# Layer 2's points by node groups in turn, and layer 3's sums and image sums on 64 rows each, with the 65th column apart

## The chip, the core and the metric

The kernel runs on one core of a Trainium2 chip. The core has five engines that work side by side, each with its own queue of instructions in fixed order: TensorE (PE, matrix products; PEld is its loading of weights), VectorE (DVE), ScalarE (ACT), GpSimd (POOL) and SyncE (SP), which here only issues DMAs. They meet by semaphores. The metric is the device time of one execution in microseconds, as the median of the runs.

## What is computed

Four graph layers run one after the other over the same 4096 nodes of 64 features and the same 4096 x 4096 matrix `adj`, which has about 0.4% nonzero entries but is handled as a full one. Between layers there is a layer norm with a ReLU and a residual sum. The code counts the layers from 0; the title's second layer is `_L1`, its third `_L2`.

```python
def _L0(h, adj):                       # layer 0
    return relu((adj @ h) @ W.T + b)

def _L1(x, adj):                       # layer 1: attention on a hyperboloid
    h = lorentz_linear(x, W, b, scale) # a "point": time = sigmoid(z0)*exp(scale)+1.1,
    q = lorentz_linear(h, Wq, ...)     #   the rest of the row scaled by
    k = lorentz_linear(h, Wk, ...)     #   sqrt((time*time-1) / sum of squares)
    att = sigmoid((2 + 2 * minkowski(q, k)) / att_scale + att_bias)
    support = (adj * att) @ h
    return support / sqrt(|inner(support)|)

def _L2(x, adj):                       # layer 2: Poincare ball
    log_ij = logmap(x_i, x_j)          # for every pair of nodes
    agg = sum_j adj[i, j] / deg_i * log_ij
    return expmap(0, agg @ weight + bias)

def _L3(x, adj):                       # layer 3: weights 2**-(rank of the neighbour)
    return (mask * 0.5 ** (k - pos)) @ (x @ weight) + bias
```

## The kernel before, in words

A tile is 128 nodes (`T` = 32 tiles). Node groups `g` = 0 and 1 are 16 tiles each; they share instructions of 128 x 1024 elements (16 tiles of 64 features).

**Layer 0 and the passage to layer 1.** For each half of the columns (`h`) and each tile of `adj_t`, TensorE (`tile0`) adds the tile's part of `adj @ h` (four f32 products on 64 array columns each, output rows 0 to 63 and 64 to 127 in turn) and counts nonzero entries for layer 3; VectorE makes the mask (`mask0`) and adds up the degrees (`degree0`, into `TB`); ScalarE turns the counts into bytes (`make_code`) and stores them. Then comes a serial passage. `update0(1)` adds the second half of layer 0's result to `X`; `norm_stats` and `norm_out` normalize both groups; `flip` turns features on TensorE, `flipped_out` copies them; `linear` multiplies with the weights; `lorentz_squares` (ScalarE), `lorentz_ratio`, `lorentz_root` and `lorentz_point` make the points h, then q, then k, each time for both groups. `high`, `key_low` and GpSimd's subtraction split q and k into two f16 parts; `fold` and `fold_both` turn these on TensorE and copies bring them back. `degrees` sums the degrees on TensorE, with idle products (`keep_at_work`) between.

**The score loop** has 64 steps `s` of two halves `u`: `scores` (TensorE), `sigm` (ScalarE), `product` with `adj` (VectorE) and `gather1` (TensorE), which adds the product's 128 x 1024 numbers into 64-row sums, again on 64 array columns in turn. Some of the folding and copying for group 1 is set into its first steps.

**Layer 2** works on 72 units `(S, p)`: a strip `S` of 512 nodes against a pair `p` of tiles (256 nodes). The distance is symmetric, so 56 units are *mirrored*: they serve the node sums of both sides. In unit n, `scores2` makes the products (f32, two row halves of the array) and `sides2` adds side terms (four row groups); ScalarE squares (`square2`), takes logarithm and two exponentials (`roots2`) and a last logarithm (`arc2`); VectorE makes `rest2`, `sum2`, `pair2`; GpSimd multiplies with `adj` (the *near* part); for a mirrored unit TensorE transposes the pair factors (`mirror2`) and VectorE multiplies these with the other block of `adj` (`far2`). The sums weight each node's row `Zn` of 65 numbers (64 features and a time part): `gather2_near` adds 2 products of 512 columns over the strip, kept in PSUM for the strip's length and brought out by `near2_out`; `gather2_far` adds 4 products of 256 columns, brought out after each unit by `far2_out` into the image `GA` (65 rows). `nodes2` turns the image back to nodes by products with the identity, 32 in all, in three groups of 8, 8 and 16 tiles; the last group comes inside layer 3's loop.

TensorE's order by iteration n is `scores2(n+1)`, `sides2(n)`, `mirror2(n-1)`, then the sums of unit n-2. VectorE's is `far2_out(n-3)`, `near2_out(n-3)` where a strip ends, `sum2(n)`, `far2(n-1)`, `rest2(n+1)`, inserted steps of the next or last passage, `pair2(n)`. ScalarE's is `roots2(n)`, inserted steps, `square2(n+1)`, `arc2(n)`. This order is written out by hand. Loads of `adj` blocks run five units ahead and wait for the sums of unit n-5.

**Layer 3** steps 64 times over the stored bytes: `power` on ScalarE and VectorE, 12 bf16 passes on TensorE (`step3`); the end of layer 2 for the last 16 tiles is set into its steps (`last_passage3`).

An f32 product is two passes of TensorE in the trace (a weight load and a stream each); a plain f32 transpose is one.

## Time and profile before

| | us |
|---|---|
| median of 3 runs | 1091.84 |
| lowest and highest run | 1090.72, 1092.6 |
| the profiled execution | 1090.43 |
| its span, from first to last instruction | 1088.7 |
| TensorE busy in the span | 1036.7 |
| VectorE busy | 862.8 |
| ScalarE busy | 767.5 |

A busy time is the time in which at least one instruction of the engine runs, so two products at once count once. The chain of waits goes back from the last instruction to what released it, and again from there. By it layer 0 ends at about 250 us, the first score product starts at 304.77, the units of layer 2 run from about 553 to 971, and the rest is layer 3.

### The profile page before, as it was taken

Reading aid. Unit: us, or ns where it says so; the run is one execution under the profiler, and the core shown is the slowest. Engines: PE = TensorE matmul, PEld = TensorE weight load, DVE = VectorE, ACT = ScalarE, POOL = GpSimd, SP = SyncE. Lnnn points to the kernel's source line nnn. Section 1 sums busy time; section 2 is a strip of 40 time slices with the busy share of each in tenths; the row PEclk is TensorE's granted clock in tenths of the full one; section 3 lists DMA queues with packets and bytes.
Section 4 is the critical chain, followed back from the end, with each engine's and each line's share of the span. In section 5 each row is a group of like instructions: output and inputs, shape, how many; then the busy total and the mean of one; then the engine's idle time right before and its main releaser. Section 6 shows DMA issues by size and latency. Waiting matters only on the chain.

```text
span 1088.7 us, 14887 instructions
## 1 busy us (share of the span) xinstructions
PE 1036.7 (95%) x5430; PEld 448.2 (41%) x5430; DVE 862.8 (79%) x1013; ACT 767.5 (71%) x807; POOL 270.7 (25%) x140
## 2 busy tenths in 40 slices
PE   7999999999789999999979999999999998989998
PEld 2333333336633333334324443444554554436544
DVE  7999989996766666697669987887789887898781
ACT  5555455553556656676688899988888888997682
POOL 1089500000010000003015364434343433440010
PEclk9999999999989999999999999999999999999999
DMA  9989989980048888778754445555455545446451
GB/s 353 396 343 423 393 322 346 359 331 30 2 154 274 280 290 280 247 274 288 245 180 136 135 135 175 177 172 193 155 168 181 170 140 174 136 140 208 140 173 40
DMA packets 96341, 238.32 MB, mean 219 GB/s; under 512 B 16400, under 2 KB 45072, under 8 KB 79888
## 3 DMA queue, kind: packets, MB, share of 16 engines
q1 hardware_dynamic: 87056, 220.62, 58.3%
q10 hardware_dynamic: 9216, 16.78, 4.0%
q8 instruction: 43, 0.70, 0.3%
q14 instruction: 26, 0.21, 0.1%
HBM read 219.55 MB, written 17.83 MB: 218 GB/s over the span
## 4 chain that ended last, share of the span: by engine, by line
PE 74%; DVE 12%; ACT 9%; issue 4%; DMA 1%; SPq 0%; DVEq 0%; ACTq 0%
PE PS L563 51%; PE PS L737 5%; PE PS L738 5%; PE PS L870 4%; PE PS L839 4%; ACT work L1224 2%; ACT work L1232 2%; DVE work L1969 2%; DVE work L1957 1%; ACT work L1235 1%; DVE ring L1975 1%; DVE work L1963 1%; ACT work L1218 1%; PE PS L575 1%; ACT work L1155 1%
## 5 line engine op out<-in xcount | busy, mean ns | idle before, releaser
L1637 DVE TENSOR_TENSOR work<-work,ring 128x1024 f32<-128x1024 f32 x128 | 151.2, 1223 | 76.8 <-ACT work L1155 76.7
L1155 ACT ACTIVATE work<-PS,att_sc 128x1024 f32<-128x1024 f32 x128 | 147.7, 1202 | 85.7 <-PE PS L738 78.4
L1090 ACT ACTIVATE work<-PS 128x1024 uint8<-128x1024 f32 x128 | 124.0, 1020 | 107.6 <-PE PS L563 107.6
L563 PE MATMUL PS<-ring,work 128*65 128x256 f32 (+1 forms) x600 | 191.8, 467 | 4.1 <-DVE work L1996 4.0
L541 POOL TENSOR_TENSOR ring<-work,ring 128x1024 f32<-128x1024 f32 x57 | 135.9, 2384 | 236.6 <-DVE work L1969 236.5
L563 PE MATMUL PS<-work 128*64 128x512 f32 (+2 forms) x800 | 153.6, 526 | 1.1 <-ACT work L1218 1.0
L1963 DVE SCALAR_TENSOR_TENSOR work<-PS,work 128x1024 f32<-128x1024 f32 x72 | 88.0, 1223 | 53.8 <-PE PS L563 45.3
L563 PEld LDWEIGHTS PS<-ring,work 128*65 128x65 f32 x600 | 80.8, 139 | 91.5 <-issue 66.0
L737 PE MATMUL PS<-work 128*128 128x512 f16 x256 | 98.9, 386 | 2.0 <-DVE work L1444 1.3
L1224 ACT ACTIVATE work<-work 128x1024 f32<-128x1024 f32 x72 | 76.0, 1055 | 34.8 <-DVE work L1957 34.7
L738 PE MATMUL PS<-work 128*128 128x512 f16 x256 | 98.2, 384 | 0.0
L1969 DVE SCALAR_TENSOR_TENSOR work<-work 128x1024 f32<-128x1024 f32 x72 | 87.9, 1221 | 2.3 <-ACT work L1239 1.8
L563 PEld LDWEIGHTS PS<-work 128*64 128x64 f32 (+2 forms) x800 | 38.2, 119 | 120.7 <-issue 112.3
L839 PE MATMUL PS<-TB,TA 64*128 64x512 f32 x288 | 81.6, 643 | 2.6 <-DVE work L1963 2.6
L1239 ACT ACTIVATE work<-work 128x1024 f32<-128x1024 f32 x72 | 75.8, 1053 | 9.1 <-DVE work L1963 6.8
L563 PE MATMUL PS<-work,TB 128*64 128x512 bf16 x672 | 76.4, 384 | 2.1 <-DVE work L1952 2.1
L1232 ACT ACTIVATE work<-work 128x1024 f32<-128x1024 f32 x72 | 76.1, 1057 | 2.3
L563 PE MATMUL PS<-work,tri_above 128*128 128x512 bf16 x256 | 75.8, 379 | 0.0
L1235 ACT ACTIVATE work<-work 128x1024 f32<-128x1024 f32 x72 | 75.0, 1042 | 0.0
L870 PE MATMUL PS<-ident,work 128*128 128x128 f32 x448 | 62.0, 282 | 13.3 <-DVE work L1969 12.5
L563 PE MATMUL PS<-work,tri_rest 128*128 128x512 bf16 x248 | 74.4, 382 | 0.0
L1500 DVE TENSOR_TENSOR TB<-TB,work 128x2048 f32<-128x2048 f32 x32 | 74.2, 2318 | 0.1
(267 smaller groups left out, 1479.9 us busy)
## 6 DMA issues: line engine op xcount, KB each, us to landing
ring<-in_adj_t SPq DMA_DIRECT2D x96, 1024.0 KB, 5.3
ring<-in_adj_t SPq DMA_DIRECT2D x104, 512.0 KB, 3.8
work<-in_adj_t SPq DMA_DIRECT2D x32, 1024.0 KB, 8.3
codes<-work ACTq DMA_DIRECT2D x64, 256.0 KB, 7.4
ring<-codes SPq DMA_DIRECT2D x64, 256.0 KB, 3.7
H<-in_adj_t SPq DMA_DIRECT2D x24, 512.0 KB, 3.9
X<-in_x SPq DMA_DIRECT2D x2, 256.0 KB, 4.5
X<-in_x SPq DMA_DIRECT2D x1, 512.0 KB, 9.9
```

The lines of the kernel that those rows point to most:

```text
L541: nc.gpsimd.tensor_tensor(near(n), sums(n), near(n), ALU.mult).then_inc(sem("near_ready"), 1)
L563: return mm(out_ap, lhsT, rhs, start=starts, stop=True, skip_group_check=True)
L737: mm(o, k_hl[:, jt * P:(jt + 1) * P], q_hh[:, i0:i0 + BANK], start=True, stop=False)
L738: ins = mm(o, k_hl[:, jt * P:(jt + 1) * P], q_ll[:, i0:i0 + BANK], start=False, stop=True)
L839: mm(z_banks(n)[:, q * BANK:(q + 1) * BANK], TA[half_rows(q), p * P:(p + 1) * P], TB[half_rows(q), S * STRIP:(S + 1) * STRIP], start=True, ...
L870: ins = nc.tensor.transpose(PS[:, c:c + P], sums(n)[:, q * BANK + i * P:q * BANK + (i + 1) * P], ident[:, :])
L1090: nc.scalar.activation(made[:, k, u * UNIT:(u + 1) * UNIT], PS[:, (4 + 2 * u) * BANK:(6 + 2 * u) * BANK], ACT.Relu).then_inc(sem("codes_ma ...
L1155: nc.scalar.activation(att[:, u, :], PS[:, (4 + 2 * u) * BANK:(6 + 2 * u) * BANK], ACT.Sigmoid, bias=att_sc[:, 2:3], scale=att_sc[:, 1:2]) ...
L1232: nc.scalar.activation(sums(n), lnr[:, n % ROT, :], ACT.Exp, scale=0.5).then_inc(sem("root_ready"), 1)
L1637: V.tensor_tensor(prob[:, m % 4, :], att[:, u, :], ring[:, s % RING, u * UNIT:(u + 1) * UNIT], ALU.mult)\
L1963: V.scalar_tensor_tensor(sums(n), z_banks(n), 1.0, sums(n), ALU.max, ALU.add)\
L1969: V.scalar_tensor_tensor(sums(n), sums(n), TAU_MAX, lnr[:, n % ROT, :], ALU.min, ALU.mult)\
```

## The change

**First part.** Layer 0's second half gets its second block of eight tiles written out, and the normalization of group 0 for layer 1 (`sums_l1`, `centre_l1`, `spread_l1`, `feats_l1`) is set between its tiles; it writes into `cen` and is flipped right after the last tile. The points then go group by group in the order h0, h1, q0 with k0, q1 with k1 (`POINTS`), with statistics of their own for k. The degrees are summed in one go. The first scores wait for q0 and k0 alone. What is left of k1 (factor, point, rounding, low part, fold) and q1 is put into steps 1 to 14 of the score loop; q1's products are copied out of PSUM first (`zq_out`).

**Second part.** The near sums use output rows 0 to 63 and the far sums rows 64 to 127, in one routine that alternates them and waits for both parts first. The 65th column is summed by products with a single weight column, near on output rows 0 and 32 and far on rows 64 and 96, into the second half of PSUM bank 3. `far2_out` and `near2_out` have two pieces each. The node images are added up by a product with two identities one above the other (`stacked`), and the 65th column of each tile by one or two products with one column of the identity. Group 1's turned left rows go through bank 0 in place of bank 3.

```diff
+            nc.gpsimd.tensor_tensor(stacked[:, :], ident[:, 0:D], ident[:, D:P], ALU.add).then_inc(sem("consts_ready"), 1)
...
+            pe.wait_ge(sem("feats_ready_l1"), 1)
+            flip(cen, 0, 0).then_inc(sem("flipped"), 1)
             pe.wait_ge(sem("sums_out0_v"), 1)
             to_nodes(wbd["l0"][:, :], UNIT, 2, 0).then_inc(sem("z0_ready"), 1)
 
             pe.wait_ge(sem("codes_made"), 4 * T)
+            pe.wait_ge(sem("flip_out"), 1)
+            linear(wbd["l1"][:, :], 1, 0, 4).then_inc(sem("lin_h"), 1)
             pe.wait_ge(sem("deg_added"), 2 * T)
...
+            degrees(7, 6)
+            for _ in range(4):
+                keep_at_work(6)
+            pe.wait_ge(sem("feats_ready_l1"), 2)
+            flip(H, 1, 0).then_inc(sem("flipped"), 1)
+            pe.wait_ge(sem("feats1_ready"), 1)
+            flip(HL, 0, 0).then_inc(sem("flipped"), 1)
             pe.wait_ge(sem("deg_out"), 1)
...
+            pe.wait_ge(sem("flip_out"), 2)
+            linear(wbd["l1"][:, :], 1, 1, 4).then_inc(sem("lin_h"), 1)
+            pe.wait_ge(sem("flip_out"), 3)
+            linear(wbd["q"][:, :], 2, 0, 4).then_inc(sem("lin_q"), 1)
+            linear(wbd["k"][:, :], 3, 0, 0).then_inc(sem("lin_k"), 1)
+            for _ in range(8):
+                keep_at_work(2)
+            pe.wait_ge(sem("feats1_ready"), 2)
+            flip(HL, 1, 0).then_inc(sem("flipped"), 1)
+            pe.wait_ge(sem("flip_out"), 4)
+            linear(wbd["q"][:, :], 2, 1, 4).then_inc(sem("lin_q"), 1)
+            linear(wbd["k"][:, :], 3, 1, 0).then_inc(sem("lin_k"), 1)
...
-                if s == 0:
+                if s == 5:
                     fold_both(1)
-                if s == 4:
+                if s == 10:
                     pe.wait_ge(sem("khl_out"), 2)
+                    fold_high(1, 2)
+                if s == 13:
+                    pe.wait_ge(sem("qhh_out"), 2)
                     fold_low(1, 2)
...
                 if n == AUX_L:
-                    pe.wait_ge(sem("far_out"), mirrors(n - 1))
-                    turn_left(1, 3)
+                    pe.wait_ge(sem("aux_r_out_a"), 2)
+                    turn_left(1, 0)
...
                 if n > AUX_R and mirrors(n) == mirrors(AUX_R) + 1:
-                    pe.wait_ge(sem("aux_r_out_a"), 2)
+                    pe.wait_ge(sem("aux_l_out"), 2)
                     pe.wait_ge(sem("aux_r_out_v"), 2)
...
+                if mirrored(n):
+                    pe.wait_ge(sem("far_ready"), mirrors(n))
+                if mirrors(n) - mirrored(n) > 0:
+                    pe.wait_ge(sem("far_out"), mirrors(n) - mirrored(n))
                 for q in range(2):
-                    ins = add(PS[0:D + 1, 2 * BANK:3 * BANK], Zn[:, 2 * p + q, 0:D + 1], near(n)[:, q * BANK:(q + 1) * BANK],
-                              opens(n) and q == 0)
-                ins.then_inc(sem("agg2_near"), 1)
-
-            def gather2_far(n):
+                    add(PS[half_rows(0), 2 * BANK:3 * BANK], Zn[:, 2 * p + q, 0:D], near(n)[:, q * BANK:(q + 1) * BANK],
+                        opens(n) and q == 0)
+                    if mirrored(n):
+                        for i in (2 * q, 2 * q + 1):
+                            add(PS[half_rows(1), 3 * BANK:LAST], Zn[:, S * ST + i, 0:D], far(n)[:, i * PAIR:(i + 1) * PAIR], i == 0)
+                for q in range(2):
+                    if mirrored(n):
+                        last_far2(n, 2 * q)
+                    for c in range(2):
+                        ins = add(PS[32 * c:32 * c + 1, LAST:LAST + PAIR], Zn[:, 2 * p + q, D:D + 1],
+                                  near(n)[:, q * BANK + c * PAIR:q * BANK + (c + 1) * PAIR], opens(n) and q == 0)
+                    if q:
+                        ins.then_inc(sem("agg2_near"), 1)
+                    if mirrored(n):
+                        ins = last_far2(n, 2 * q + 1)
+                        if q:
+                            ins.then_inc(sem("agg2_far"), 1)
+
+            def last_far2(n, i):
                 S, p = UNITS[n]
...
+                for c in range(2):
+                    ins = add(PS[64 + 32 * c:65 + 32 * c, LAST:LAST + P], Zn[:, S * ST + i, D:D + 1],
+                              far(n)[:, i * PAIR + c * P:i * PAIR + (c + 1) * P], i == 0)
+                return ins
...
                 for t in range(*GROUPS[q]):
-                    ins = mm(PS[:, agg2_col(t):agg2_col(t) + D + 1], GA[0:D + 1, t * P:(t + 1) * P], ident[0:D + 1, 0:D + 1],
-                             start=True, stop=True)
+                    r, to = (P, stacked) if t >= ST else (D, ident)
+                    mm(PS[:, agg2_col(t):agg2_col(t) + D], GA[0:r, t * P:(t + 1) * P], to[0:r, 0:D], start=True, stop=True)
+                    for k, (r, rows) in enumerate(last_rows(t)):
+                        ins = add(PS[:, agg2_col(t) + D:agg2_col(t) + D + 1], rows, ident[:, r:r + 1], k == 0)
...
+            flipped_out(0, 0)
+            lorentz_squares("h", 4, 0)
+            one("ln_sq", grp(sqr, 1), grp(cen, 1), ACT.Square, ("ln_centred", G + 3))
+            power_of("ln_sd", st[2], st[1], -0.5, "ln_var", G + 2, (1,))
+            lorentz_roots(("h", 0))
+            flipped_out(0, 1)
+            flipped_out(1, 0)
+            lorentz_squares("h", 4, 1)
+            lorentz_squares("q", 4, 0)
+            lorentz_roots(("h", 1))
+            lorentz_squares("k", 0, 0)
+            flipped_out(1, 1)
+            lorentz_roots(("q", 0), ("k", 0))
+            lorentz_squares("q", 4, 1)
+            lorentz_squares("k", 0, 1)
+            high("q", HBq(0), Q2(0), 0)
+            high("k", HBk[0], grp(K2, 0), 0)
             folded_out("qhh_out", q_hh, 0, 4, "qhh_ready")
...
+            lorentz_sum("h", 1)
+            lorentz_ratio(("h", 1))
+            lorentz_sum("q", 0)
+            feature_point(1)
+            lorentz_sum("k", 0)
+            lorentz_ratio(("q", 0), ("k", 0))
...
                 if s == 1:
+                    lorentz_factor(("k", 1))
+                    key_point(0, 1)
+                if s == 3:
+                    key_low(1)
+                if s == 6:
                     keys_out(1)
-                if s == 4:
+                if s == 7:
+                    lorentz_factor(("q", 1))
+                    query_point(1, HBq(1))
...
+                    V.tensor_tensor(at, at, got, ALU.add)
+                    V.tensor_tensor(last, last, last_got, ALU.add).then_inc(sem("far_out"), 1)
```

## Rows read from the trace of the kernel before

**Rows 1.** The page's first part: busy us (share), instructions, of each engine.
```profile
PE 1036.7 (95%) x5430; PEld 448.2 (41%) x5430; DVE 862.8 (79%) x1013; ACT 767.5 (71%) x807; POOL 270.7 (25%) x140
```

**Rows 2.** Busy times by stretch; window: length, each engine, clock, DMA share, GB/s.
```profile
158.00:250.00 92.00, 92.00 (x400) 29.45 (x397) 85.89 (x50) 47.95 (x51) 0.00 (x0) 1.00 0.88 325
250.00:305.00 55.00, 42.54 (x385) 36.24 (x384) 37.85 (x108) 27.20 (x44) 2.27 (x2) 0.93 0.02 6
574.00:635.00 61.00, 59.62 (x271) 27.55 (x271) 57.42 (x79) 52.76 (x58) 31.29 (x22) 0.98 0.46 147
635.00:690.00 55.00, 50.11 (x280) 22.62 (x279) 41.93 (x47) 52.07 (x54) 27.70 (x13) 0.97 0.47 154
690.00:771.00 81.00, 81.00 (x391) 39.54 (x390) 63.91 (x76) 70.18 (x71) 33.22 (x14) 1.00 0.54 177
771.00:911.00 140.00, 138.02 (x684) 70.77 (x682) 116.30 (x163) 118.23 (x129) 54.21 (x25) 1.00 0.50 162
971.00:1088.00 117.00, 106.50 (x904) 58.42 (x902) 77.49 (x127) 77.78 (x91) 7.87 (x3) 0.99 0.44 145
```

**Rows 3.** The chain of waits in one mirrored unit: start us, us, what.
```profile
689.28 3.44 PE PS L563 x12
692.72 1.06 PE PS L839 x4
693.78 0.33 PE PS L563 x4
694.11 1.02 PE PS L870 x8
```

**Rows 4.** The chain of waits in the passage to the scores, and one ScalarE copy.
```profile
283.26 0.91 PE PS L597 x8
284.19 1.02 ACT work L1118
285.24 1.20 DVE st L1559
...
286.61 0.32 DVE time_q L1566 x2
...
301.58 1.88 PE PS L715 x16
303.49 1.24 DVE work L1444
304.77 0.61 PE PS L737
...
299.86 1.86 ACT L1043 ACTIVATE work<-PS 128x2048 f16<-128x2048 f16 x1
```

**Rows 5.** Groups by shape: score loop on VectorE and ScalarE; busy, mean ns, idle before.
```profile
L1637 DVE TENSOR_TENSOR work<-work,ring 128x1024 f32<-128x1024 f32 x128 | 151.2, 1223 | 76.8 <-ACT work L1155 76.7
L1155 ACT ACTIVATE work<-PS,att_sc 128x1024 f32<-128x1024 f32 x128 | 147.7, 1202 | 85.7 <-PE PS L738 78.4 <-DVE work L1637 7.1
```

**Rows 6.** Instructions in time on TensorE: one tile's sums in layer 1.
```profile
390.62 1.94 PE L563 MATMUL PS<-work 128*64 128x512 f32 x8
```

**Rows 7.** Instructions in time on ScalarE: first step of two following units.
```profile
681.17 1.06 ACT L1224 ACTIVATE work<-work 128x1024 f32<-128x1024 f32 x1 [0.22 <-DVE work L1957]
686.34 1.06 ACT L1224 ACTIVATE work<-work 128x1024 f32<-128x1024 f32 x1 [0.22 <-DVE work L1957]
```

**Rows 8.** Groups by shape: VectorE bringing out far and near sums.
```profile
L1985 DVE TENSOR_TENSOR work<-work,PS 65x256 f32<-65x256 f32 x42 | 17.3, 411 | 4.4 <-PE PS L563 4.4
L1996 DVE TENSOR_TENSOR work<-work,PS 65x512 f32<-65x512 f32 x11 | 7.5, 679 | 0.4
```

**Rows 9.** TensorE: one-column products in time, then the last node images in the chain.
```profile
270.47 1.62 PE L662 MATMUL PS<-ones,TB 128*128 128x1 f32 x14
...
982.26 3.72 PE PS L957 x32
```

**Rows 10.** Waits from 965 us on: who waited for whom, total us, times, longest.
```profile
ACT work L1246 <- PE PS L957: 3.1, 1, 3.1
```

More of the change, by code:

```diff
@@ L213, in graph_layers @@
         HL = nodes(slot(5))
-        HBk = nodes(slot(7))
+        HBk = [work[:, k * UNIT:(k + 1) * UNIT].rearrange("p (t c) -> p t c", t=TG) for k in (14, 6)]
         def HBq(g):
@@ L698, in fold, with fold_high @@
                 return ins
-            for g in range(G):
+            def fold_high(g, dst):
                 pe.wait_ge(sem("q_high"), g + 1)
-                fold(Q2, 0, g, 4 + 2 * g).then_inc(sem("qhh_ready"), 1)
+                fold(Q2, 0, g, dst).then_inc(sem("qhh_ready"), 1)
             def fold_low(g, dst):
@@ L980, in _ @@
                 if n >= 2:
[L981 to L983 removed]
+                    gather2(n - 2)
                 if n in FLIPS:
@@ L1213, in second_half2 @@
                 if n == AUX_L + 1:
-                    one("aux_l_out", aux_l[:, UNIT:2 * UNIT], banks(3, 4).bitcast(BF16), ACT.Copy, ("aux_turned", 4))
+                    one("aux_l_out", aux_l[:, UNIT:2 * UNIT], banks(0, 1).bitcast(BF16), ACT.Copy, ("aux_turned", 4))
             def square2(n):
@@ new lines, in lorentz_factor @@
+            def lorentz_factor(*points):
+                for n, (tag, g) in enumerate(points):
+                    ratio, root, factor = (grp(v, g) for v in TAGS[tag][2:5])
+                    dve.wait_ge(sem("point_root"), nth(tag, g))
+                    chained(n, V.reciprocal(factor, root))
+                for n, (tag, g) in enumerate(points):
+                    ratio, root, factor = (grp(v, g) for v in TAGS[tag][2:5])
+                    hold(n)
+                    chained(n, V.tensor_tensor(factor, factor, ratio, ALU.mult))
+                for n, (tag, g) in enumerate(points):
+                    ratio, root, factor = (grp(v, g) for v in TAGS[tag][2:5])
+                    hold(n)
+                    chained(n, V.tensor_tensor(factor, factor, root, ALU.add))
```

296 lines of the change are left out of this document (158 added, 138 removed).

## The prediction

> **What bounds the kernel now.** I read the page's engine line first: TensorE is busy 95% of the span [rows 1]. A busy share says little where stages differ, so next the busy times by stretch [rows 2], then in each stretch what is late last. The end of layer 0 (158 to 250 us) has TensorE without a gap and VectorE at 85.89 of 92. Between 250 and 305 us nothing is full: a serial passage. From 574 to 635 TensorE (59.62 of 61) and VectorE (57.42) are both nearly full. From 635 to 690 ScalarE is (52.07 of 55). From 690 to 771 TensorE alone is (81.00 of 81). From 771 to 911 TensorE again, with VectorE near it in parts. The last layer starts near 971 and TensorE leads there too.
>
> One unit of layer 2 is visible in the chain of work [rows 3]: sums 3.44 us, distance products 1.06, side terms 0.33, mirror transposes 1.02, together 5.85. Nothing else stands in that chain.
>
> **Part one, the passage from layer 0 to the scores.** Today the chain runs from about 250.2 to the first score product at 304.77 [rows 4], 54.5 us. Prices [rows 4]: a full-size vector step 1.20 to 1.22 (reduce, scaling), a pair of 16-column steps 0.32 (I take 0.2 for a lone one), a ScalarE pass 1.02, a bank of products 0.91 and some 0.2 of bias ahead (I take 2.4 for a group of two banks with its latency), a fold 1.88 on a TensorE that has just idled (I take 1.0 on one that has not), a copy of folded rows 1.24 on VectorE and 1.86 on ScalarE. The new order, step by step: flip of the features of group 0, then second half of layer 0's products, 3.3 (ends 253.5). Update, mean, centring of group 1, the sum of h0, spread of group 1: five full steps and a little, 6.3 (259.8). Ratio of h0 (seven small steps) 1.6, reciprocal root 0.8, features 1.2, factor 0.7, point 1.4: 5.9 (265.7). Flip of group 1, copy, product 4.7 (270.4). Square, sum, ratio, sum of q0, factor, point of h1: 7.2 (277.6). Flip, copy, products of q1 and k1: 6.8 (284.4). ScalarE squares k1 before it rounds q0, so that waits: square, rounding, fold, copy 5.1 (289.5). Low parts and key fold with copies 3.4 (292.9). The chain is 42.7 us, 11.8 less; with folds at 1.88 each 2 less gain. I take 11. What leaves the chain runs inside the score loop: a fold on TensorE, which is full there, costs 1.0. The vector steps (factor and point, 2.2 at tiles 1 and 7, low part 1.2) and ScalarE's (roundings 1.0, copy 1.9) meet idle times of 76.8 and 85.7 us over 64 tiles [rows 5], 1.2 and 1.3 a tile, and two of four product buffers in hand: nothing. Without that cover each would cost its own length, about 9 in all.
>
> The normalization of group 0 moves into layer 0's second half: four full vector steps and six small, 6.2 us, into 6.1 us of vector idle time [rows 2]. The masks run over two tiles ahead of TensorE, about 8 us, so a lag of 5 is not felt; behind it stand only the releases of eight load buffers. I take nothing, at worst 2. The constant added on GpSimd comes before TensorE's first work, which still waits later for features. **Sum: -10, between -6 and -12.**
>
> **Part two, a mirrored unit's sums.** 56 of the 72 units are mirrored. Today 12 passes (each f32 product is two), 4096 columns, one after the other: 3.44 us, 0.84 ns a column [rows 3]. New: near on array columns 0 to 63 and far on 64 to 127. In layer 1 sums of just that form, 8 passes of 512 columns, take 1.94 in place of 3.44 [rows 6], so pairs run at once, four slots of 0.43 with a tail. So 1.72 to 1.93 here, since the two sides have unequal passes. The 65th column: near 8 passes of 256, far 16 of 128, on four column groups. If four run at once 8 x 256 x 0.84 / 2 = 0.86; if one after the other 3.44; if two at once 1.72. Nearest are the side terms, four products at once on four row groups in 0.33 [rows 3]: I take 0.9 to 1.1. The side terms stream 512 two-byte columns each, which at half the f32 price is 0.22, and take 0.33 [rows 3]: I charge the 0.1 to the change of array form, and there are two more such changes in the new unit.
>
> The Trainium skill, TensorEngine Tiling (Restrictions), states that changing the tiling mode drains the engine, which speaks against this change; the 0.1 above is what the trace shows of it, and it is in the sum. By TensorE: Matmul & The Clock Gate (Part 3) three column groups gave 2.38 times, which for the 65th column would be an estimated 0.86 x 3 / 2.38 = 1.08.
>
> Together 2.8 to 3.3, taken as 3.0: a unit on TensorE goes from 5.85 to 5.4. The next limit is the ring sum, far product, root argument on VectorE, then logarithm and root on ScalarE: where TensorE isn't late, ScalarE's first step recurs after 686.34 - 681.17 = 5.17 us [rows 7]. So the gain can't pass 0.68 a unit.
>
> **Its costs.** VectorE takes a second piece out for each. 65x256 takes 411 ns and 65x512 679 [rows 8]: 1.05 ns a column, so 0.28 for 128, and 0.21 queued; 0.3 for the near side. An unmirrored unit's sums grow from 1.72 by 0.86 and two changes of form, 1.3 with the seams. The merged sums wait for near, far and the former far output at once; all three are done during the products and transposes ahead, and behind the wait stand only the next unit's products. At unit 14 the turned rows now leave over bank 0, so a mirror waits for one more ScalarE copy: 1.0 once. The node images: 32 passes take 3.72 now, 0.116 each, and one-column passes take the same, 14 in 1.62 [rows 9], since they load 128 columns of weights. A tile past the fourth needs six passes in place of two: the groups grow by 2.8, 3.7 and 7.4.
>
> **By stretch** [rows 2]. 574 to 635: VectorE gets 10 x 0.21 + 0.3 on 57.42 and has 3.6 idle, partly TensorE's doing: +0.5. 635 to 690: unmirrored sums six times 1.3 on a TensorE with 4.9 idle, plus the copy: +2.5. 690 to 771: 81 / 5.85 = 14 units x 0.45: -6.3. 771 to 911: TensorE -0.45 x 22 + 2.8 + 3.7 = -3.4, VectorE 22 x 0.21 + 0.6 = +5.2 where its extra steps make it last: -1. 911 to 971 has both kinds of unit, six of each kind, and no engine far ahead: 0. Tail: the last two units are unmirrored, 2.6, and the last images 7.4. ScalarE already waits 3.1 for those images [rows 10], TensorE's following steps queue behind them, and TensorE is 106.50 of 117 there, so nothing covers: +10. **Sum: +5.7**, between -2 and +10.
>
> **Total.** -10 + 5.7 = -4.3 on 1088.7 of span, 1090.43 with what lies around it: 1086.1. The runs' median 1091.84 is 1.4 above the profiled execution; the same difference on the median gives 1087.5.
>
> **Rivals.** (1) *The array doesn't run the 65th column's four groups at once.* The trace has no one-column product on column groups. At 1.72 to 1.85 for it a unit takes 6.2 to 6.4: some 45 mirrored units that are TensorE's +0.4 to +0.5, -10 + 10 + 20 + 3 (unmirrored) and the images' 6.5 partly: about 1112, slower. It decides from sums of 3.5 us a unit upwards. For it: passes of unequal length, short ones with a load each. Against: [rows 3, 6]. Chance 13%. A page's rule would make it worse: if products start strictly in order and a product's second pass waits for its own columns, near's second pass blocks far's first; the layer 1 sums would then take five slots, 2.15 and its tail, where 1.94 is seen [rows 6]. A unit would take 6.8 and the kernel about 1130; 3%. (That products keep strict order is the Trainium skill, TensorE: Matmul & The Clock Gate, Part 3.)
> (2) *The passage gains half.* ScalarE's queue is in fixed order and serves two groups; each late square or rounding holds the next, and the new chain passes through it seven times. Then -5 in place of -10: 1092.5, no change or slightly slower. 16%.
> (3) *Sums at 2.8 and a TensorE that hasn't slowed at the first scores*: -12, -8.5 and a freer TensorE from 771 on: 1080. 12%.
> (4) Forecast, 1087.5, own range 1083 to 1092: 56%.
>
> **How the numbers follow.** No change is within 0.2% (2.2 us), about what a measurement of this kernel can tell. Of the forecast's 56% I count 41 faster, 10 the same, 5 slower; (3) 12 faster; (2) 2 faster, 7 same, 7 slower; (1) 16 slower. Faster 0.55, same 0.17, slower 0.28. Range 1079 to 1108: it takes in (3), (2) and the milder part of (1).
>
> **What would show it.** First score product at 292.9 to 295, and a score loop of the old length but for one fold. In the steady stretch a period of 5.2 to 5.5 with sums of 2.8 to 3.3; above 3.44, rival 1. The 128-column vector pieces at 0.28. Last node images 11.1. The end of the loop of units earlier by some 14, the total by 4. The prediction is wrong if units get longer, if TensorE waits for masks before 250, or if the tail hides the images.

## The result and the profile after

The changed kernel takes 1110.95 us (median of 4 runs, 1110.51 to 1112.73) where the kernel before takes 1092.22 in the same comparison: a ratio of 1.0175, 95% interval 1.0156 to 1.0193. It is slower by 19 us; forecast was 1087.5. The profiled execution has a span of 1109.3 us, 20.6 more than the span before.

The page of the changed kernel, its first parts (busy us, share of the span, instructions; then TensorE's granted clock, the share of full speed at which the engine was allowed to run, in tenths over 40 slices), to be set against [rows 1]:

```profile
span 1109.3 us, 18109 instructions
PE 1043.4 (94%) x6983; PEld 481.0 (43%) x7002; DVE 887.1 (80%) x1080; ACT 768.6 (69%) x808; POOL 250.1 (23%) x141
PEclk9999999999899999999989999999999899997999
```

No engine's share has moved by more than a point or two, which is why a page of shares can't tell where 20 us went. Milestones can. I took the starts of the first score product, of the last attention product, and, in layer 2, of ScalarE's logarithm of the sums, once per unit (unit n runs from the start before it to its own; the time between is called its period here). The tail is what follows the last of them. From the two traces, in us:

| stretch | before | after | difference | forecast |
|---|---|---|---|---|
| start and layer 0, to the last mask | 239.3 | 242.1 | +2.8 | 0 |
| passage, last mask to first score product | 65.5 | 54.7 | -10.8 | -10 |
| scores to the first unit | 253.9 | 254.3 | +0.3 | 0 |
| units 1 to 24 | 136.8 | 143.5 | +6.7 | +3.0 |
| units 25 to 38 | 82.0 | 73.9 | -8.1 | -6.3 |
| units 39 to 60 | 139.3 | 152.5 | +13.2 | -1 |
| units 61 to 71 | 56.9 | 57.3 | +0.4 | 0 |
| tail | 115.0 | 131.0 | +16.0 | +10 |

The loop of units was to end some 14 us earlier. Its last logarithm starts 4.6 us later (978.3 after, 973.7 before).

Both gains are there. The steady mirrored unit has a period of 5.17 us in place of 5.85. TensorE's lines in time of one such unit after (start us, us, instruction), to be read against [rows 3]:

```profile
697.32 1.09 PE L903 MATMUL PS<-ident,work 128*128 128x128 f32 x8
698.34 2.92 PE L591 MATMUL PS<-ring,work 128*64 128x512 f32 x36
701.19 1.13 PE L872 MATMUL PS<-TB,TA 64*128 64x512 f32 x4
702.25 0.39 PE L591 MATMUL PS<-work 9*128 9x512 bf16 x4
702.58 1.09 PE L903 MATMUL PS<-ident,work 128*128 128x128 f32 x8
703.60 2.71 PE L591 MATMUL PS<-H,work 128*64 128x512 f32 x28
```

The sums take 2.85 us from their start to the start of the distance products, where they took 3.44. The products of the 64 features take 1.88 of it, and the 65th column 0.97, from 700.22 on; two groups at a time would be 1.72 by the prediction's count. In the trace the first products on its four column groups start at 700.217, 700.223, 700.230 and 700.237, so the four do run side by side. The largest losses lie elsewhere: in the node images. Their stretches after, by windows (length, then busy us of each engine with instructions, granted clock, DMA share, GB/s), are the first group's, the second's, the last's, and the 25 us behind the last:

```profile
770.40:775.90 5.50, 5.50 (x42) 5.18 (x38) 1.49 (x3) 2.83 (x3) 2.36 (x1) 0.91 0.63 194
877.20:883.70 6.50, 6.50 (x50) 6.50 (x46) 2.29 (x4) 3.02 (x3) 2.36 (x1) 0.77 0.50 161
989.20:1006.10 16.90, 16.90 (x99) 16.86 (x97) 3.35 (x6) 0.00 (x0) 0.00 (x0) 0.62 0.52 169
1006.10:1031.00 24.90, 24.90 (x201) 13.92 (x202) 18.83 (x39) 20.15 (x27) 0.00 (x0) 0.91 0.39 124
```

and in the kernel before the last group's, whose end [rows 9] also show:

```profile
982.20:986.00 3.80, 3.80 (x36) 3.73 (x36) 3.28 (x6) 0.72 (x1) 0.00 (x0) 1.00 0.83 257
```

TensorE has no gap in any of them, and yet its granted clock averages 0.62 in the last. The tiles in time show the fall itself (changed kernel, last images; two products of 64 columns, four of one column, for each tile):

```profile
991.93 0.41 PE L1006 MATMUL PS<-stacked,work 128*128 128x64 f32 x2
992.18 0.56 PE L591 MATMUL PS<-ident,TA 128*128 128x1 f32 x4
992.60 0.41 PE L1006 MATMUL PS<-stacked,work 128*128 128x64 f32 x2
992.85 0.56 PE L591 MATMUL PS<-ident,TA 128*128 128x1 f32 x4
...
994.51 0.67 PE L1006 MATMUL PS<-stacked,work 128*128 128x64 f32 x2
994.97 0.96 PE L591 MATMUL PS<-ident,TA 128*128 128x1 f32 x4
995.79 0.67 PE L1006 MATMUL PS<-stacked,work 128*128 128x64 f32 x2
```

A tile takes 0.67 us (six passes of 0.112) up to 993.3 and 1.28 behind it: from 2.4 to 1.2 GHz. The images take 16.9 us in all, where 16 tiles at 0.67 would be 10.7.

### The profile page after: what moved, and what is told of

It is laid out like the page before. It is cut to its first block, busy times and chain, and to the rows that moved or that the text cites. A ratio compares the mean times of both kernels' runs of the same rounds, so it can differ in the third digit from the quotient of the medians.

```text
span 1109.3 us, 18109 instructions
## 1 busy us (share of the span) xinstructions
PE 1043.4 (94%) x6983; PEld 481.0 (43%) x7002; DVE 887.1 (80%) x1080; ACT 768.6 (69%) x808; POOL 250.1 (23%) x141
## 4 chain that ended last, share of the span: by engine, by line
PE 55%; issue 21%; POOL 13%; DVE 5%; ACT 4%; DMA 1%; POOLq 0%; SPq 0%; DVEq 0%; ACTq 0%
PE PS L591 39%; POOL ring L569 10%; PE PS L767 5%; PE PS L768 5%; POOL H L569 2%; ACT work L1213 1%; PE PS L603 1%; DVE work L2095 1%; DMA X<-in_x 1%; PE PS L625 1%; PE PS L1006 1%; PE PS L694 0%; DVE work L2089 0%; PE PS L725 0%; PE PS L919 0%
## 5 line engine op out<-in xcount | busy, mean ns | idle before, releaser
L591 PE MATMUL PS<-ring,work 128*1 128x128 f32 (+3 forms) x1800 | 172.9, 369 | 6.5 <-DVE TA L2114 3.1
L591 PEld LDWEIGHTS PS<-ring,work 128*1 128x1 f32 (+1 forms) x1800 | 89.3, 102 | 82.5 <-issue 53.5
L591 PEld LDWEIGHTS PS<-work 128*64 128x64 f32 (+2 forms) x800 | 38.2, 119 | 121.0 <-issue 112.2
L1282 ACT ACTIVATE work<-PS 128x1024 f32<-128x1024 f32 x72 | 72.6, 1009 | 5.0 <-PE PS L591 4.9
```

Source lines behind the costliest of these rows:

```text
L591: return mm(out_ap, lhsT, rhs, start=starts, stop=True, skip_group_check=True)
```

## The experiments

Each kernel ran against the kernel before, which took 1092.62 to 1093.63 us in these later comparisons; the ratios are to that. Periods below are in us; they are those of the profiled execution. A unit's period repeats from one kernel to the next within some 0.03 us where nothing touched it and the clock is the same (unit 4 is an exception, below), so single units can be compared. "39+40" and "55+56" hold the first two groups of images and the unit behind each.

| kernel | time | ratio, interval | 1-24 | 25-38 | 39+40 | 55+56 | tail |
|---|---|---|---|---|---|---|---|
| before | 1092.22 | | 136.8 | 82.0 | 13.44 | 13.13 | 115.0 |
| changed | 1110.95 | 1.0175 (1.0156-1.0193) | 143.5 | 73.9 | 18.59 | 20.14 | 131.0 |
| passage_only | 1083.71 | 0.9911 (0.9887-0.9935) | 137.7 | 81.9 | 13.44 | 13.14 | 113.4 |
| sums_only | 1124.38 | 1.0294 (1.0277-1.0311) | 142.6 | 73.9 | 18.94 | 20.13 | 131.1 |
| merged_images | 1092.66 | 0.9994 (0.9978-1.001) | 143.8 | 73.9 | 13.81 | 13.27 | 122.7 |
| dense_images | 1138.98 | 1.0421 (1.0403-1.0439) | 143.8 | 73.9 | 25.43 | 25.50 | 143.1 |
| held_images | 1105.49 | 1.012 (1.0087-1.0154) | 143.8 | 73.9 | 21.82 | 17.02 | 125.4 |
| merged_no_adds | 1086.76 | 0.9948 (0.9928-0.9967) | 142.2 | 73.5 | 13.88 | 13.21 | 120.9 |
| merged_turn | 1091.74 | 0.9987 (0.9967-1.0007) | 141.9 | 73.9 | 16.58 | 13.27 | 121.0 |
| merged_x1 | 1089.22 | 0.9976 (0.9945-1.0008) | 141.6 | 73.9 | 15.17 | 13.27 | 121.1 |
| passage_held | 1081.81 | 0.9883 (0.9857-0.9908) | 137.6 | 81.9 | 13.45 | 13.13 | 113.4 |
| passage_held_long | 1081.17 | 0.9885 (0.9867-0.9903) | 136.6 | 81.9 | 13.44 | 13.14 | 113.4 |

**The two parts alone.** passage_only has the new order of the second layer's points and nothing of the sums. None of its lines for the units of layer 2 differs from the kernel before.

> The kernel before with the second layer's points by groups alone; the third layer's sums, image sums and the turn of unit 14 as before. In the changed kernel the first score product came 10.9 us earlier counted from the last mask of layer 0, and the last attention product of layer 2 came 7.7 us earlier than before; layer 0 itself and the kernel's start were 2.8 us longer together. My theory: this part is a gain of its own and is kept to the end, as the rest follows it without slack: 1092.2 - 7.7 = 1084.5 if the lost 2.8 us belong to it, 1081.7 if they belong to the other part (ratio 0.990 to 0.993). Rival: the gain is given back behind the scores, as the units of the third layer meet a VectorE that still has the moved work: 1089 to 1092. In layer 0 I expect the extra 1.7 us to show here (the normalization's steps between the masks), and the first 1.1 us not to.

sums_only is the reverse: every line on the 65th column, `stacked`, and the turn into bank 0.

> The kernel before with the other part alone: third layer's sums and image sums on 64 rows each, with the 65th column apart, and the turn of unit 14 into the other bank. If the two parts add up, this is 1111 + 8 = 1119 (ratio 1.024 to 1.027), with the steady period of the units at 5.17 us, the unit of the first image group at 12.1 us and the last image group at 16.9 us, as in the changed kernel. Rival: the loss in the changed kernel came from the two parts together (the moved points of layer 2 against the first units of layer 3): then this is under 1110.

passage_only came out as the theory had it: 1083.71, ratio 0.9911. sums_only is far from its rival, but at 1124.38 it is 5 us over the 1119 expected, and its ratio of 1.0294 lies above the range given. Its profiled execution, the shortest of its four (1121.54 us), has the expected periods and last images of 17.3 us; why the other three took 1124 to 1125 no profile shows. Multiplied, the parts give 0.9911 x 1.0294 = 1.020 beside 1.0175, which agree within their intervals. The passage is a gain of 9 us, the sums are a loss of 32. One more expectation fell: the 1.7 us of layer 0 were to show in passage_only and not in sums_only. From first to last mask the trace of before has 227.7 us, the changed one 229.4, passage_only 230.4, and sums_only, which touches nothing in layer 0, 229.2. merged_turn, which has the new layer 0, has 227.7 again. So most of the 2.8 us at the start is the spread of executions, not the change.

**The images' products.** merged_images lets near row and far row of a tile share a block of columns; in the gather the two near rows take alternate tiles, and the images read both values, for two tiles, with one product:

```diff
-                        ins = add(PS[32 * c:32 * c + 1, LAST:LAST + PAIR], Zn[:, 2 * p + q, D:D + 1],
-                                  near(n)[:, q * BANK + c * PAIR:q * BANK + (c + 1) * PAIR], opens(n) and q == 0)
+                        ins = add(PS[32 * c:32 * c + 1, LAST:LAST + PAIR].rearrange(...), Zn[:, 2 * p + q, D:D + 1],
+                                  every_other(near(n)[:, q * BANK:(q + 1) * BANK], c), opens(n) and q == 0)
...
-                    for k, (r, rows) in enumerate(last_rows(t)):
-                        ins = add(PS[:, agg2_col(t) + D:agg2_col(t) + D + 1], rows, ident[:, r:r + 1], k == 0)
+                    if t % 2:
+                        ins = add(PS[:, at:at + D + 2:D + 1], GU[p // NS][:, p % NS * P:(p % NS + 1) * P], stacked[:, 0:D:32], True)
```

> The changed kernel with the 65th column laid out so that the near row and the far row of a tile share one block of columns; a pair of tiles then gets its two values of the column from one product with two columns, in place of eight passes of one column. My theory: the one-column products of the images let TensorE's granted clock fall to half (0.77 and 0.70 in the two units with images, 0.50 in most of the last group, 0.82 to 0.91 in the units behind). Three passes per tile at 0.116 us and the clock held: last group 5.6 us in place of 16.9, first group's unit with its follower 5.4 us shorter, second 7.0 us shorter: 1111 - 23.7 = 1087.3 (range 1085 to 1091), granted clock 1.00 in these units. Rival: the number of passes alone counts and the clock falls as before, since one-column products are left: each of the losses is halved: 1111 - 12 to 13 = 1098. Rival: the images aren't the cause: 1108 to 1111.

Measured 1092.66, 18 us less than the changed kernel, where the theory had 23.7 and the first rival 12 to 13. That lies between the two and above the theory's range of 1085 to 1091. Windows of its three groups of images:

```profile
776.80:779.90 3.10, 3.10 (x29) 2.92 (x25) 1.54 (x3) 2.87 (x3) 2.11 (x1) 1.00 0.53 163
878.50:881.20 2.70, 2.70 (x28) 2.66 (x24) 2.32 (x4) 2.67 (x3) 0.93 (x1) 1.00 0.50 139
983.30:991.10 7.80, 7.80 (x52) 7.76 (x50) 3.37 (x6) 0.00 (x0) 0.00 (x0) 0.70 0.93 297
```

The first two groups hold the full clock and their units with followers shrink by 4.8 and 6.9 us, as expected (5.4 and 7.0). The last took 7.8 and not 5.6: its clock fell to 0.70. It has few one-column products left, so "one-column products" was too narrow a name for the cause. The passage took 60.7 us in the profiled execution in place of 54.7 (below), and the median seems to carry some of that: of its ten executions the five with a mean clock of 0.980 to 0.983 took 1093.8 to 1096.7 us, the five with 0.986 or 0.987 took 1088.8 to 1091.5. In all four profiles of kernels with merged images the last group fell (6.4 to 8.0 us up to the next product), and in two of them the first group's stretch did as well (39+40 of 16.58 and 15.17 us). So merging makes the fall rarer and shorter and doesn't end it.

**Which work holds the clock.** dense_images repeats each product of 64 columns:

```diff
-                    mm(PS[:, agg2_col(t):agg2_col(t) + D], GA[0:r, t * P:(t + 1) * P], to[0:r, 0:D], start=True, stop=True)
+                    for _ in range(3):
+                        mm(PS[:, agg2_col(t):agg2_col(t) + D], GA[0:r, t * P:(t + 1) * P], to[0:r, 0:D], start=True, stop=True)
```

> The changed kernel with each 64-column image product issued three times in a row (the same value written again), the one-column products as they are. More work of TensorE, only denser. My theory (the clock falls for lack of dense work): at full clock a tile takes 0.67 + 0.43 = 1.10 us in place of 1.28 at the lower clock: last group 17.6 us, first two groups' units 14.0 us each, the units behind back at 5.2 us: 1111 to 1113 in all, granted clock at least 0.9 in these units and 1.00 behind them. Rival (the clock falls for another reason, whatever TensorE does there): ten passes at the lower clock, 2.1 us per tile: last group 30 us, in all 1130 or more, with the granted clock as low as in the changed kernel.

The theory in that form was wrong, and the time is the rival's: 1138.98 us. Its last group, by window:

```profile
1009.30:1037.50 28.20, 28.20 (x160) 28.16 (x158) 3.37 (x6) 0.00 (x0) 0.00 (x0) 0.61 0.30 101
```

TensorE's weight loads (second of the busy numbers) fill 28.16 of these 28.20 us. Products of 64 columns are thin too: each loads 128 columns of weights to stream 64. That gave the theory its second form, and the next kernel its test: long products between the tiles, in a corner of a bank that the images leave free (one more stands behind each group).

```diff
                         ins = add(PS[:, agg2_col(t) + D:agg2_col(t) + D + 1], rows, ident[:, r:r + 1], k == 0)
+                    for _ in range(2):
+                        mm(PS[:, spare:spare + PAIR], tri_rest[:, :], tri_above[:, :].unsqueeze(1).broadcast_to([P, 2, P]),
+                           start=True, stop=True)
```

> The changed kernel with two further products of 256 columns and 128 weight rows each behind every tile of the images (their result is used by nobody). In dense_images more products of 64 columns made the stretch longer and the clock lower still (0.60 to 0.69), so my theory in its first form, that the one-column products alone starve the clock, fell. Second form: what starves it is a stretch made of products of 64 columns and fewer, in which TensorE mostly loads weights; long products between them should hold the clock, although they are more work. Then a tile takes 0.67 + 0.21 = 0.88 us at the full clock: last group 14.1 us (16.2 in the changed kernel), first two units with images 12.2 us each (12.1 and 13.0), the units behind them 5.2 to 5.6 us (6.5 and 7.1), granted clock 0.95 or more in all of these: 1111 - 6 = 1105 (range 1102 to 1108). Rival: the clock falls in this stretch whatever is added: a tile takes 1.28 + 0.42 = 1.70 us behind the fall, last group 24 us: 1125 or more.

Measured 1105.49, 5.5 us less than the changed kernel, by a kernel that gives TensorE over 64 products more. Windows of its three groups and of the 25 us behind the last:

```profile
771.00:778.60 7.60, 7.60 (x56) 6.53 (x52) 1.53 (x3) 2.86 (x3) 2.36 (x1) 0.82 0.44 141
881.10:887.20 6.10, 6.10 (x65) 6.01 (x61) 2.28 (x4) 3.00 (x3) 2.37 (x1) 1.00 0.53 172
989.60:1002.10 12.50, 12.50 (x126) 12.29 (x124) 3.35 (x6) 0.00 (x0) 0.00 (x0) 1.00 0.66 229
1002.10:1027.00 24.90, 24.90 (x220) 14.40 (x220) 19.87 (x44) 21.34 (x28) 0.00 (x0) 1.00 0.44 138
```

In the second and last group the clock stays at 1.00 and the stretch gets shorter with more in it (16.9 to 12.5 us). In the first it fell all the same (0.82), and that unit and its follower are 3.2 us longer than in the changed kernel; the dose that is enough isn't settled by these runs. The second form holds in two groups of three. The time fell on the 1105 expected partly by luck: the last group took 12.5 us where 14.1 were given, the first unit with images 14.84 where 12.2 were.

The rival that the clock falls there whatever TensorE does is refuted by the second and last group. What is left of the theory's words needs care, though: weight loads fill 12.29 of the 12.50 us in the last group too, so their busy share doesn't tell a stretch that holds its clock from one that doesn't. What differs between the kernels is the long products between the thin ones.

**VectorE's second pieces.** merged_no_adds drops the additions of the 65th column on VectorE (its products and its first copies stay), so that column of the means is incomplete.

```diff
                     V.tensor_tensor(at, at, got, ALU.add)
-                    V.tensor_tensor(last, last, last_got, ALU.add).then_inc(sem("far_out"), 1)
```

> The kernel with merged images, with the additions of the 65th column into its sums left out on VectorE (48 of 0.29 us and 4 of 0.41 us; its copies and TensorE's products stay), so the 65th column of the third layer's means is not what it should be. Theory: VectorE's second pieces are what made units 4 to 21 and 41 to 51 longer than in the kernel before, since VectorE is busy 93 to 99% there; each piece that ends on the path gives back its 0.29 us: some 25 of them, -7 us against merged_images: 1085.5. Rival: what made these units longer is that the far sums are now taken up only behind the near sums and the other way round (two waits where there was one), and the pieces are hidden: within 2 us of merged_images, 1090 to 1093.

Measured 1086.76, 5.9 us under merged_images (5.0 by the ratios). But of the two traces' difference of 10.2 us, 3.4 lie before the first score product, 2.7 of them in the passage. Counted in periods, units 1 to 24 give 1.6 us (1.15 of it unit 4, which differs from one profile to the next in any case, below), units 41 to 54 give 2.2, mostly 0.2 each, and the tail 1.8, where the last images' clock differed too. So the additions cost about the 0.2 us they were priced at, in the units where VectorE is last, and they are not what made most of units 4 to 21 longer. Neither is the rival shown: these units had other reasons, found in the next two kernels.

**The turn of unit 14.** In the changed kernel, waits from 640 to 645 us (who waited for whom, total us, times, longest):

```profile
PE PS L903 <- ACT work L1091: 2.3, 1, 2.3
DVE H L2101 <- PE PS L903: 2.0, 1, 2.0
```

The mirror waits for ScalarE's copy out of bank 0, and VectorE for the mirror. merged_turn gives that copy to VectorE:

```diff
-                if n == AUX_L + 1:
-                    one("aux_l_out", aux_l[:, UNIT:2 * UNIT], banks(0, 1).bitcast(BF16), ACT.Copy, ("aux_turned", 4))
...
+                if n == AUX_L + 1:
+                    copy_out("aux_l_out", aux_l[:, UNIT:2 * UNIT], banks(0, 1).bitcast(BF16), ("aux_turned", 4))
                 sum2(n)
```

> The kernel with merged images, with the copy of the turned side vectors of unit 14 made by VectorE ahead of the sum of unit 15, in place of ScalarE behind its other work. The turn now lies in bank 0, where the next unit's mirror is written, so in the changed kernel the mirror of unit 15 waited for ScalarE's copy until 643.58 us and VectorE stood idle 1.96 us before it could take it. Theory: this wait is the whole of what the move of the turn costs: units 14 to 16 together go from 19.06 us to 17.1 to 17.6 us (the kernel before has 17.12 us), and the time from 1092.7 to 1091. Rival: the three units are longer for VectorE's further pieces, and the copy on VectorE adds its 0.68 us: 19.1 to 19.7 us, 1092.7 to 1093.3.

Units 14 to 16 take 6.58 + 5.27 + 5.55 = 17.40 us where merged_images has 19.05, inside the theory's 17.1 to 17.6: the wait was 1.65 us of the stretch. The time, 1091.74, is within the noise of 1092.66.

**GpSimd and VectorE.** In unit 6 the period rose from 5.89 to 7.32 us. VectorE and GpSimd there, changed kernel:

```profile
581.24 2.37 POOL L533 TENSOR_TENSOR X<-X,work 128x1024 f32<-128x1024 f32 x1
581.79 2.37 DVE L2083 TENSOR_SCALAR work<-work 128x1024 f32<-128x1024 f32 x1
```

and the same two operations in the kernel before, with the next one of VectorE:

```profile
587.69 4.14 POOL L505 TENSOR_TENSOR X<-X,work 128x1024 f32<-128x1024 f32 x1
587.78 0.68 DVE L1957 TENSOR_SCALAR work<-work 128x1024 f32<-128x1024 f32 x1
588.38 1.22 DVE L1969 SCALAR_TENSOR_TENSOR work<-work 128x1024 f32<-128x1024 f32 x1
```

Before, VectorE's scaling started 0.09 us behind the addition, and the addition took the longer time, 1.77 us more than 2.37; VectorE's scaling and its next product fill 1.82 us there, up to 589.60. After, it started 0.55 us behind, and its 0.68 became 2.37: it ended 0.55 us behind the addition. merged_x1 (made from merged_turn) has the addition on VectorE, in unit 6:

```diff
-                if n == 4:
-                    add_x1("support_used", 2)
...
+                    V.tensor_tensor(grp(X, 1), grp(X, 1), grp(cen, 1), ALU.add).then_inc(sem("x1_added"), 1)
```

> The kernel merged_turn with the addition of the second half's residual (X, 1024 columns) made by VectorE in unit 6, in place of GpSimd's behind unit 4. In every kernel with the new sums VectorE's scaling in unit 5 (0.68 us elsewhere) took 2.36 to 2.37 us while GpSimd's addition of 2.37 us ran; in the kernel before, that addition itself took 4.14 us and VectorE's scaling there 0.68 us. Theory: the two engines' operations can't run side by side, and the new sums shift their starts by the tenths of a us that decide which of them waits: without GpSimd's addition the scaling takes 0.68 us again, units 5 and 6 together go from 14.08 us to 11.9 to 12.6 us, and unit 7 takes up to 1.2 us more: 0.5 to 1.5 us shorter in all, within the spread of the runs (1090 to 1092). Rival: units 5 and 6 are longer for the further VectorE pieces and the scaling only ended late for another reason: still 14.0 or more, plus 1.2 us for the addition on VectorE.

VectorE's scaling is back at its length:

```profile
576.09 0.68 DVE L2080 TENSOR_SCALAR work<-work 128x1024 f32<-128x1024 f32 x1
```

Periods of units 5 and 6 go from 14.08 to 12.39 us, exactly the 1.69 us that the scaling had gained, and unit 7 takes 1.26 more for the addition: -0.43 in all. The whole time can't show that (1089.22, its interval overlaps merged_turn's); the periods do. The wait for GpSimd is shown by this; as a gain in time the edit is next to nothing.

**The passage's own clock.** In the profiles of the kernels with the new passage as it is (merged_x1 among them) it took 54.7, 54.7, 54.7, 56.4, 57.9, 60.7, 61.2 and 61.2 us. In passage_only (61.2), windows of the degree sums; the second line is the fall (the sums take 4.6 us longer there than in the changed kernel, and most of the rest of the 6.5 us is lost at the products of q1, where the clock falls again):

```profile
258.80:262.00 3.20, 3.20 (x31) 3.06 (x30) 3.12 (x5) 2.14 (x3) 0.00 (x0) 1.00 0.02 5
262.00:272.20 10.20, 10.20 (x55) 9.20 (x56) 6.35 (x21) 0.86 (x4) 0.00 (x0) 0.59 0.00 1
```

The change joined the two halves of the degree sums (32 tiles of one-column products) and left one long product to four passes, where the kernel before has one to two, but for its 14 passes in a row [rows 9]. passage_held puts one behind each tile again:

```diff
-                    if t % 2 == 0:
-                        keep_at_work(spare)
+                    keep_at_work(spare)
...
-            for _ in range(4):
-                keep_at_work(6)
```

> The passage part alone, with a long product behind every tile of the degree sums in place of every second one, and the four behind them dropped (12 more in all, 2.5 us of TensorE at the full clock). In three of four profiles of kernels with this part the granted clock fell to 0.5 from 264 to 272 us, in the degree sums (one-column products with one long product to four passes; the kernel before has one to two), and the first score product came 60.7 to 61.2 us behind the last mask in place of 54.6. Theory: the thinner mixture lets the clock fall in most executions; with the denser one it holds at 1.00 from 257 to 285 us, and the passage takes 54.6 + 2.5 = 57 us: 1082 to 1085 with less spread than the 8 us of passage_only's runs. Rival: the fall isn't set by the degree sums: passage of 61 us or more, 1086 to 1090.

> The kernel of passage_held again, with more runs, since its runs and those of passage_only spread over 7 to 8 us (1079.7 to 1086.7, 1080.8 to 1089.1) and neither interval tells the two apart. Theory: the clock holds in the degree sums in all of its executions and the rest of the spread is that of layer 0 and of the fold stage behind: median 1081 to 1083.5, ratio 0.987 to 0.991. Rival: the 1081.8 was luck and it is the same as passage_only: 1083.5 to 1085.5.

Its clock held in the degree sums in both profiles; in the second:

```profile
263.00:273.00 10.00, 9.67 (x82) 8.78 (x82) 6.32 (x24) 2.33 (x6) 0.00 (x0) 1.00 0.00 1
```

and its passages took 57.6 and 57.2 us. passage_held_long, the same kernel once more, has four runs: 1081.17 us (1080.17 to 1082.86), ratio 0.9885 (0.9867 to 0.9903). This is the fastest kernel of the study, faster than before and than the changed one. Its time isn't steady either: the profiled execution of passage_held took 1086.74 us with the clock held in the degree sums, and lower at other places (0.85 from 300 to 320). That it beats passage_only (0.9911) isn't shown, as the intervals overlap; the profiles show only that the 61 us didn't return in two executions.

## Why the prediction was wrong

The forecast was -4.3 us on the profiled execution, the result is +20.6 (1110.99 against 1090.43), a miss of 24.9 us: about 13.9 by the images' clock, 6.4 by a sum over unlike units, 3.7 in the first units, 2.8 at the start (no step of mine; most of it spread, as sums_only shows), 0.7 in the score loop and the last units, less 1.8 and 0.8 by which the steady units and the passage beat their terms. By steps:

**The passage: right.** -10.8 against -10. The first score product came at 296.7, where 292.9 to 295 was given, since layer 0 ended 2.8 later in this execution. What was missing is that the new passage comes in two lengths: rival 2's "half the gain" occurs (passage_only's 61.2 is -4.3), but mostly through the clock of the degree sums and not through ScalarE's queue.

**The steady unit: right, at its limit.** Sums 2.85 (2.8 to 3.3 given), period 5.17 where 5.4 was taken and 5.17 named as the floor, -8.1 in place of -6.3. Rival 1, the array running the four groups one after the other, is refuted by the 2.85 and by the four starts within 0.02 us; its strict form too. The time fell near rival 1's 1112 by chance: its mechanism isn't there. Nor do that rival's terms add up to 1112: -10 + 10 + 20 + 3 on 1091.84 are 1115 before any part of the images.

**The node images: the step that failed.** The count of passes was right, and so was their price at the full clock, 0.112 us for 0.116 taken [rows 9]. The exception are the first four tiles: they have four passes and still take 0.66 us each (770.38 to 773.01), some 0.8 in all over the price; their products use 64 and 128 weight rows in turn, but no run tests whether that is why. But I carried a price from stretches of 1.62 and 3.72 us to one of 11 us and never asked what TensorE's clock does in a long stretch of thin products. At 0.67 a tile the last group would take 10.7 us and takes 16.9: 6.1 lost, with the change to the next product.

For the first two groups an estimate goes by merged_images, which held its clock in both. Its units 39 to 60 take 140.2 us. Its images take 3.36 and 2.99 us up to the next product; eight tiles at 0.67 would take 5.4 each, 4.5 more in all. That gives 144.7, and the changed kernel takes 152.5: 7.8 more, which I put down to the clock, 0.8 of it in units 41 and 57. Together 13.9 of the 24.9 us. Without them the time would be near 1097, inside the range. "Last node images 11.1" was the line that would show it, and it did. That the shape of these products is the cause is shown by merged_images and held_images; what share of long products is enough stays open.

The Trainium skill, TensorE: Matmul & The Clock Gate (HAM oscillation — how this bites in real kernels), gives as the abstract rule that TensorE must have no long idle gaps. By that sentence alone nothing should happen here. In this trace the clock falls without a gap: 16.90 of 16.90 us busy, clock 0.62.

**Units 39 to 60: a sum over unlike units.** I offset the images' +6.5 against a gain of 22 x 0.45 for TensorE, with VectorE's +5.2 as the smaller of two rivals for last place: -1. The units turned out to take turns: those where VectorE is last (46, 48 to 51: +0.2 to +0.7 each) lose, those with a free VectorE gain 0.2 to 0.5 (43 to 45, 52, 53, 59). The forecast needed -7.5 from all units of this stretch but the four with images. They came to +1.1, 0.8 of it the clock's. Without the clock's 7.8 us the stretch is +5.4 in place of -1: 6.4 us of the miss. Taken unit by unit from the trace of before, with periods from 5.6 to 7.3 us, it could have been seen.

**Units 1 to 24: 3.7 over the forecast.** Part of this is arithmetic: six times 1.3 less 4.9 of idle time, with 1.0 for the copy, are 3.9, and the forecast used 2.5. The move of the turn cost 1.9 us (units 14 to 16: 17.12 to 19.06, and merged_turn gives 1.65 of it back), where 1.0 was taken: the mirror waited 2.3 us for the copy, which ScalarE makes between the steps of its own unit. The meeting with GpSimd's addition costs 1.69, which no step of mine had. Unit 4 has 1.1 more at a clock of 0.76 (before 0.79), and 6.66 to 7.84 in the other kernels with the new sums at 0.73 to 0.80. The mean clock alone doesn't order these (6.66 and 7.57 both at 0.76); how much of it is the change stays open. Units 10 and 11 have 1.4, where VectorE brings out four pieces at a strip's end, copies among them that no experiment took away; that these are the cause is argued, not shown.

**VectorE's pieces: right in price.** Groups by shape, changed kernel:

```profile
L2113 DVE TENSOR_TENSOR work<-work,PS 64x256 f32<-64x256 f32 x42 | 17.8, 424 | 2.5 <-PE PS L591 1.3
L2114 DVE TENSOR_TENSOR TA<-TA,PS 33x128 f32<-33x128 f32 x36 | 10.4, 288 | 0.0
```

288 ns each (0.28 forecast). The cost goes by the columns, not the rows: 64x256 takes 424 ns where 65x256 took 411, so two pieces cost more than one.

**The tail.** The gathers of the last two units: from unit 71's logarithm to the first image 8.5 us before, 11.0 after, +2.5 where 2.6 was given. The images +13.1, where 7.4 was given. Nothing hides either, as forecast.

## What to carry to other kernels

Price small products at both clocks (here 0.112 and 0.21 us a pass). A long stretch of thin products (64 columns streamed, or one, for each load of 128) looks fully busy and yet ran partly at half the clock here, and the work behind it paid too; the price from a short stretch doesn't hold in a long one. Merging such products (here two rows and two tiles in one, 18 us) gave more than adding long ones between them (5.5 us). And where a stretch holds units with different engines last, add the costs up unit by unit; an average over the stretch lets gains in one kind of unit pay for losses in another, which the kernel doesn't do.

## What the runs showed of the hardware

Long products between thin ones held TensorE's clock at 1.00 over 12.5 us in the last group, where without them it averaged 0.62 over 16.9 (in the first group it fell to 0.82 in spite of them); more thin ones made it no better (0.61 over 28.2). Whether the fall comes can differ between profiles of the same instructions (a passage of 54.7 or 61.2 us; 39+40 of 13.81 or 16.58, in different kernels), and it seems to within one kernel: passage_only's four executions took 1089.13, 1085.22, 1082.21 and 1080.82 us at mean clocks of 0.984, 0.984, 0.990 and 0.990.

VectorE's scaling of one operand (0.68 us) took 2.37 us beside a GpSimd addition, which came first by 0.55 us; when it was later by 0.09 us only, the addition took 4.14 us in place of 2.37. The Trainium skill, SBUF — State Buffer (Who interferes with whom), has a port pair shared by the two engines as an exclusive lock: whoever issues first gets it for the whole instruction, and the other is fully blocked. The blocking agrees with both traces: VectorE's scaling was late by 1.69 us where the addition had 1.82 to go, and the addition by 1.77 where VectorE's two operations take 1.82. Who wins agrees in the changed kernel alone; before, the addition starts first by the profile and yet is the one that waits, and a difference of 0.09 us may be less than the profile can tell.

Four column groups with passes of unequal length did run side by side, f32 products of two passes among them: 36 passes of sums in 2.85 us, where 12 took 3.44, the last 24 of them on four groups in 0.97.
